# Second attention: VectorE's heads written out, the joining sum on GpSimd, quotients formed in the last stage

## What is computed

```
xn = layernorm(x)
q, k, v = split(xn @ w_qkv)                 # B = 4, N = 256 in the reference's names; here 1 x 2048 rows, 16 heads of 64
out = softmax(rotate(q) @ rotate(k).T / 8) @ v          # per head
x = x + out @ w_out + b_out + ffn(xn)
ffn: h = silu(xn @ w1 * s1) * (xn @ w2 * s2)
     h = gelu(h @ h1 * s); h = gelu(h @ h2 * s); h @ w3 * s3
```

## Time and profile before

| | before |
|---|---|
| median of 3 runs | 3438.32 us |
| profiled execution | 3422.39 us |
| its span, first to last instruction | 3420.6 us |
| PE busy | 2997.9 us (88%) |
| DVE busy | 2827.3 us (83%) |
| ACT busy | 3045.0 us (89%) |
| POOL busy | 2475.8 us (72%) |

### The profile page before, as it was taken

How to read it: one execution, slowest core, us unless ns; L and a number is a source line. 1 busy time by engine, 2 the same in 40 slices (tenths; PEclk the granted TensorE clock), 3 DMA queues, 4 the chain that set the end, 5 groups by cost and what they waited for, 6 DMA issues and landing times. The chain is left out here.

```text
span 3420.6 us, 60293 instructions
## 1 busy us (share of the span) xinstructions
PE 2997.9 (88%) x19523; PEld 1263.5 (37%) x19523; DVE 2827.3 (83%) x4260; ACT 3045.0 (89%) x3039; POOL 2475.8 (72%) x1581
## 2 busy tenths in 40 slices
PE   6888888888888888888887978998989889899899
PEld 3222122212222122221222434555555555555547
DVE  7989999999998999999998988887878778788321
ACT  3999999999999999999997766998989889899942
POOL 5888888888888888888875545576767667677650
PEclk9788778877788778877787989999999999999999
DMA  2000000000000000000001360110000111000000
GB/s 74 7 8 7 7 0 7 7 7 2 5 7 7 7 0 7 7 7 0 7 10 40 130 192 26 40 37 26 26 26 26 32 39 32 26 26 26 23 20 13
DMA packets 59521, 85.32 MB, mean 25 GB/s; under 512 B 10064, under 2 KB 45904, under 8 KB 58960
## 3 DMA queue, kind: packets, MB, share of 16 engines
q1 hardware_dynamic: 59344, 82.93, 8.4%
HBM read 52.31 MB, written 30.54 MB: 24 GB/s over the span
## 5 line engine op out<-in xcount | busy, mean ns | idle before, releaser
L1266 POOL TENSOR_TENSOR lo<-pr,hi 128x1024 f16<-128x1024 f32 x384 | 820.3, 2163 | 388.5 <-ACT hi L1438 384.0
L1327 DVE TENSOR_REDUCE mx<-mx_ps 128x1 f32<-128x512 f32 x1024 | 661.3, 685 | 157.8 <-PE mx_ps L1491 156.7
L1461 ACT ACTIVATE pr<-s_ps 128x1024 f32<-128x1024 f32 x512 | 534.6, 1044 | 130.3 <-PE s_ps L1522 116.8
L1438 ACT ACTIVATE hi<-pr 128x1024 f16<-128x1024 f32 x512 | 551.0, 1077 | 0.0
L713 ACT ACTIVATE wt<-wt,theta_bias 128x2048 f32<-128x2048 f32 (+2 forms) x160 | 482.5, 3016 | 3.7 <-DVE wt L563 3.0
L722 ACT ACTIVATE wt<-wt 128x2048 f32<-128x2048 f32 x256 | 485.3, 1896 | 0.5
L501 POOL TENSOR_TENSOR wt<-base,wt 128x1024 f32<-128x1024 f32 x192 | 455.7, 2373 | 16.0
L501 POOL TENSOR_TENSOR wt<-vb,wt 128x1024 f32<-128x1024 f32 x192 | 455.4, 2372 | 16.0
L1541 PE MATMUL pv_ps<-vh,hi 128*128 128x129 f16 x4096 | 427.8, 221 | 34.7 <-DVE lo L1371 25.6
L1491 PE MATMUL mx_ps<-ka,qa 128*128 128x512 f16 x1024 | 367.6, 389 | 72.7 <-DVE mx L1327 57.9
L1541 PE MATMUL pv_ps<-vh,lo 128*128 128x65 f16 x4096 | 413.9, 193 | 0.0
(11 more groups left out here) (210 smaller groups left out, 5114.8 us busy)
## 6 DMA issues: line engine op xcount, KB each, us to landing
qk<-stg SPq DMA_DIRECT2D x6, 2048.0 KB, 10.8
vh<-v SPq DMA_DIRECT2D x16, 520.0 KB, 3.4
qa<-qk SPq DMA_DIRECT2D x16, 512.0 KB, 3.6
ka<-qk SPq DMA_DIRECT2D x32, 256.0 KB, 4.8
v<-v_st SPq DMA_DIRECT2D x3, 2080.0 KB, 7.9
qst<-parts_dram SPq DMA_DIRECT2D x144, 32.0 KB
kst<-parts_dram SPq DMA_DIRECT2D x144, 32.0 KB
qk<-stg SPq DMA_DIRECT2D x4, 1024.0 KB, 7.8
```

What stands on the lines that cost most here:

```text
L1266: eng.tensor_tensor(lo[:, i % NHL, :, :], pr_slot(i), hi[:, i % NHL, :, :], ALU.subtract).then_inc(lo_done, 1)
L1327: eng.tensor_reduce(mx4[:, q // NCH, q % NCH:q % NCH + 1], mx_ps[:, q % 2, :], AX.X, ALU.max)\
L1438: eng.activation(hi[:, i % NHL, :, :], pr_slot(i), ACT.Copy).then_inc(hi_done, 1)
L1461: eng.activation(pr_slot(i), s_ps[:, i % 2, :, :], ACT.Exp, scale=SM).then_inc(exp_done, 1)
```

## The change

Four edits. The DVE loop over pairs of heads, and POOL's loop over heads, are Python loops now, so that their streams are written out in full. The joining sum is POOL's: it reads `sums` and writes `attn1`, and it stands in POOL's queue behind the low part of steps 5, 13, 21 and 23; ACT's `take` waits for it and for the reciprocal. ACT's `divide` is gone. The reciprocals of all heads are kept (`rden`, 128 x 16 x 16), and DVE multiplies each row tile of `attn1` by them in the last stage, in 16 instructions of 128 x 1024, before the transposes. So that memory allows it, `h1` (8 KB in each partition) isn't kept through the attention any more but fetched at the start of the last stage, ahead of `h2`, `w3` and `wo`.

```diff
@@ stage_attention1, sync @@
-                                 (sb["sc"][:, 2, :], io["h1_s"]), (sb["sc"][:, 3, :], io["h2_s"]),
-                                 (sb["h1"][:, :, :], io["h1_t"].rearrange("(k p) o -> p k o", p=P))):
+                                 (sb["sc"][:, 2, :], io["h1_s"]), (sb["sc"][:, 3, :], io["h2_s"])):
@@ vector, take @@
                     eng.wait_ge(sums_taken, n_ + 2)
-                    eng.reciprocal(rden[:, :].unsqueeze(2), sums[:, :, HD1:HD1 + 1])
-                    eng.tensor_tensor(sums[:, :, 0:HD1], sums[:, :, 0:HD1], sums[:, :, HD1 + 1:VN], ALU.add)\
-                       .then_inc(div_ready, 1)
+                    eng.reciprocal(rden[:, c * TS:(c + 1) * TS, h:h + 1], sums[:, :, HD1:HD1 + 1])\
+                       .then_inc(rden_ready, 1)
@@ vector @@
-                with eng.Fori(1, H // 2 - 1) as g:
+                for g in range(1, H // 2 - 1):
                     one(g, 0)
                     one(g, 1)
@@ gpsimd @@
-                with eng.Fori(0, H) as h:
-                    for i in range(STEPS):
-                        if not on_vector(i):
-                            low(eng, h, i, lo_gpsimd)
+                def join(h, c):
+                    eng.wait_ge(sums_taken, NS * h + c + 2)
+                    eng.tensor_tensor(attn1[:, c * TS:(c + 1) * TS, h * HD1:(h + 1) * HD1], sums[:, :, 0:HD1],
+                                      sums[:, :, HD1 + 1:VN], ALU.add).then_inc(attn_ready, 1)
+                for h in range(H):
+                    for i in range(NLG):
+                        low(eng, h, i, lo_gpsimd)
+                        if i % KP == SUM + 1 and h + i // KP >= 1:
+                            join(h if i >= KP else h - 1, (i // KP - 1) % NS)
+                    join(h, NS - 2)
+                join(H - 1, NS - 1)
@@ scalar @@
-                def divide(h, c):
-                    eng.wait_ge(div_ready, NS * h + c + 1)
-                    for j in range(TS):
-                        last = eng.activation(attn1[:, c * TS + j, bass.ds(h * HD1, HD1)], sums[:, j, 0:HD1],
-                                              ACT.Identity, scale=rden[:, j:j + 1])
-                    last.then_inc(attn_ready, 1)
                 def take(h, c):
                     eng.wait_ge(attn_ready, NS * h + c + 1)
+                    eng.wait_ge(rden_ready, NS * h + c + 1)
@@ stage_output @@
+                sp.dma_start(h1[:, :, :], io["h1_t"].rearrange("(k p) o -> p k o", p=P)).then_inc(h1_loaded, 16)
@@ gpsimd @@
-                eng.wait_ge(weights_loaded, 16 * 7)
+                eng.wait_ge(h1_loaded, 16)
                 split(h1, h1_hl, 0)
@@ vector, behind the 16 casts of L1802 @@
+                for k in range(NT):
+                    by_head = attn1[:, k, :].rearrange("p (h e) -> p h e", h=H)
+                    eng.tensor_tensor(by_head, by_head, rden[:, k, :].unsqueeze(2).to_broadcast([P, H, HD1]),
+                                      ALU.mult).then_inc(divided, 1)
@@ tensor, turn @@
+                    eng.wait_ge(divided, k + 1)
```

More of the change, by code:

```diff
@@ L1232, in stage_attention1 @@
         mrow = t("mrow", [NT, P], F16)
-        sums, rden = t("sums", [P, TS, VN]), t("rden", [P, TS])
+        sums, rden = t("sums", [P, TS, VN]), sb["rden"]
         s_ps = ctx.enter_context(nc.psum_tensor("s_ps", [P, 2, 2, SC], F32))
@@ L1243, in stage_attention1 @@
         pv_done = sem("pv_done1")
-        sums_taken, div_ready, attn_ready = sem("sums_taken"), sem("div_ready"), sem("attn_ready1")
+        sums_taken, rden_ready, attn_ready = sem("sums_taken"), sem("rden_ready"), sem("attn_ready1")
         rest_loaded, v_loaded = sem("rest_loaded"), sem("v_loaded")
@@ L1463, in one @@
                             take(h - 1 if i == SUM else h, (i // KP - 1) % NS)
-                        if i % KP == SUM + 2 and not (first and i == SUM + 2):
-                            divide(h - 1 if i == SUM + 2 else h, (i // KP - 1) % NS)
                         if i >= 1 or not first:
@@ L1470, in one @@
                         take(h, NS - 1)
-                        divide(h, NS - 1)
                 one(0, first=True)
@@ L1589, in _ @@
                 eng.sem_inc(attn_ready, 1)
+                eng.sem_inc(rden_ready, 1)
                 eng.sem_inc(mrow_loaded, 16)
@@ L1605, in stage_output @@
 def stage_output(nc, io, sb):
-    base, attn1, xn2T, ident = sb["base"], sb["attn1"], sb["xn2T"], sb["ident"]
+    base, attn1, rden, xn2T, ident = sb["base"], sb["attn1"], sb["rden"], sb["xn2T"], sb["ident"]
     MO = INNER // P
@@ L1620, in sem @@
             return ctx.enter_context(nc.semaphore(name))
-        w1, w2, h1, sc = sb["w1"], sb["w2"], sb["h1"], sb["sc"]
+        w1, w2, sc = sb["w1"], sb["w2"], sb["sc"]
+        h1 = t("h1", [P, M1, F1])
         h2 = t("h2", [P, M1, F1])
@@ L1639, in stage_output @@
         low_ready, h_high, h_split = sem("low_ready1"), sem("h_high"), sem("h_split")
-        turned, aT_ready = sem("turned_e"), sem("aT_ready")
+        turned, aT_ready, divided = sem("turned_e"), sem("aT_ready"), sem("divided")
         loaded, weights_loaded = sem("loaded_e"), sb["weights2_loaded"]
+        h1_loaded = sem("h1_loaded")
         gate_ps, up_ps, sil_ready = sem("gate_ps1"), sem("up_ps1"), sem("sil_ready1")
@@ L1665, in _ @@
             def _(eng):
-                eng.wait_ge(weights_loaded, 16 * 7)
+                eng.wait_ge(weights_loaded, 16 * 6)
                 for k in range(NM):
@@ L1840, in program @@
         with ExitStack() as layer1:
-            sb |= dict(attn1=keep(layer1, "attn1", [P, NT, INNER]), w1=keep(layer1, "w1", [P, F1]),
+            sb |= dict(attn1=keep(layer1, "attn1", [P, NT, INNER]), rden=keep(layer1, "rden", [P, NT, H]), w1=keep(layer1, "w1", [P, F1]),
                        w2=keep(layer1, "w2", [P, F1]), sc=keep(layer1, "sc", [P, 4, M1]),
-                       h1=keep(layer1, "h1", [P, M1, F1]),
                        weights2_loaded=layer1.enter_context(nc.semaphore("weights2_loaded")))
```

## The result

After the change the kernel takes 3348.84 us (median of 4 runs, 3346.46 to 3351.49), beside 3432.65 us before on the same chip (4 runs, 3424.49 to 3439.79): ratio 0.9759, 95% interval 0.9736 to 0.9782. That is 84 us off where 101 were forecast, and 3349 where 3337 was. The profiled executions say more: 3346.5 us against 3322 forecast in that frame.

What follows compares the result with a forecast made beforehand. In a head PE paces steps 2 to 26, ACT the rest. 40.8 + 44.8 + 2.1 + 2.0 + 14.3 + 0.6 - 0.5 - 3.2 = 100.9 us off: 3321.5 profiled, plus 16: 3337; range 3308 to 3370.

Steps and rivals of the forecast that it cites:

- The loop written out: DVE's loop over heads: five backward branches go with the stops behind them, 40.8 us off.
- The join off DVE: Heads 1 to 14: PE's three waits behind joins lose 3.2 us a head, 44.8 off, bounds 22 and 53.
- 2.1 and 2.0 beside it: 2.1 us off in the 72.16 us head with the 3.93 us join; 2.0 off for two joins in head 0.
- The join on POOL: Heads 1 to 14: a join takes 0.75 us on POOL, ends 0.5 and 1.6, hidden, 0 lost.
- That just closes: In a head POOL needs 24 x 2.14 + 3 x 0.75 = 53.6 us before weigh(23), which PE wants at 53.65.
- The rival of POOL's pace: weigh(23) waits for POOL, a head takes 63.6 + 3X for a join of X; 3361 us at 1.3, chance 0.13.
- The division: Step 30 on ACT, heads 0 to 14: 0.95 us each, 14.3 off, other end 6; steps 6, 14, 22 nothing.
- What is late next: Head start: ka's landing holds PE's first bank up to 0.5 us, taken in by PE's 0.75 us wait before weigh(0).
- The head of 65.9 us: Forecast length of each of 14 heads: 70.07 - 3.2 - 0.95 us.
- The last stage, +3.2: h1 lands 5.6 us after the stage's start, PE's seventh gate comes 3.2 us later, bounds 2.2 and 5.6.
- The 16 multiplications: Last stage, DVE: 1.2 us each, 19.4 in all, under PE's 41.6 us of the second hidden layer, 0 lost.
- the waits change owner: PE's waits go half to DVE's reciprocal and ka's landing; 22 + 8 less gained, 3367 us, chance 0.10.

Runs made afterwards that it cites:

- e2_low_first: The changed kernel with VectorE's last low half of the head before made ahead of the first bank of maxima in step 2; 3331.15 us, ratio 0.9722.
- e3_pause: The changed kernel with four small activations, results unused, put back on ScalarE in step 30 where the division was; 3344.24 us, ratio 0.9768.
- e5_q_split: e2_low_first with the load of qa cut in two, only its first 512 columns ahead of ka on the queue; 3324.52 us, ratio 0.9682.

## Why the prediction was right, and where it was short

The range held the time and the direction was clear; the size was 17 us short in the medians and 25 in the profiled frame. By its own steps:

- **The loop written out, 40.8.** Right in its reason: no "issue" wait is left on DVE, and head 1 was a fair sample of straight code. Alone it gave 26 us of span, because three heads turned long by a late load and the collision, and one by a long join and a lower clock; without those 12 us it is 38.4.
- **The join off DVE, 44.8 with 22 and 53 as ends, and 2.1 and 2.0 beside it.** Right: 41 by ratios, 52 by spans for putting it back, though with the division gone and the loop written out, so that the joins fall elsewhere.
- **The join on POOL, nothing lost at 0.75.** Right, and for more than the stated reason. "That just closes" was too narrow: low parts come every 2.09 us (eight in 16.7) and not 2.14, a join every 0.60. So 24 x 2.09 + 3 x 0.60 = 52.0 where 53.6 was reckoned, and with two joins each it still closes by 0.7. The rival of POOL's pace, 63.6 + 3X, falls by the doubled join: its threshold lies above 1.2 us of join, not at the 0.77 at which it gives 65.9. The same 1.6 us explains, I think, most of head 15, which was 3 us shorter where none was forecast; no run tested that.
- **The division, 15 x 0.95.** This is the step that fell short. Its price is right (67.00 against 66.05 with and without). So is the remark that the load of ka would come 0.5 late and that the wait of step 4 takes it in: that much of the ka wait cost nothing in e2_low_first. It left out two things. The first stands between the two. "What is late next" was asked of PE alone. The same 0.95 us brings POOL's first low part forward, which waits only for ACT, while DVE's last low half waits behind a bank that waits for a load that doesn't move with ACT: the load is issued when the scores end and lands when it lands. Before, DVE was 0.31 us ahead of POOL; so much, and not the 0.5 of PE, was the room. Past it DVE's half took 1.99 us in place of 0.69, and the head became 67.86 and not 65.9. The pause on ACT that made the heads shorter shows it without any edit to DVE or the load. The second is the load itself: the forecast took its landing, 4.9 us after the issue, from one head. In the changed kernel the later of the two loads of ka lands 4.9 to 6.6 us after its issue, and the trace of before already had 4.8 to 6.3, those above 5.3 all in heads in which DVE stopped at its branch. Over 13 heads 28.4 us are missing (885.05 less 13 x 65.9): the order gave back 15.8 of them, the earlier load 8.4 more, and 4.2 stay open. The first two together are twice what the division was worth in these heads.
- **The head of 65.9 us.** Met, at 66.05 to 66.2, by six heads of 13 once the order of the two instructions is fixed, and by ten once the load comes earlier too.
- **The last stage, +3.2.** A misread row. The seventh gate needs product 4, but 3257.64 in the earlier trace rows is the sixth gate of the stage; the seventh comes a pair, 1.72 us, later. 3260.9 less 3259.4 is 1.5, and 1.59 was measured. Part of that match is luck: in the changed kernel, as before, the first pairs of gates ran at a granted clock of 0.67, so PE came late to the seventh. In e2_low_first, e3_pause and e5_q_split they ran at 1.00, and the same wait is 3.46 to 3.56 us.
- **The 16 multiplications, nothing.** Right, 1.27 us each and no wait behind them.

The rival "the waits change owner" named the right kind (ka's landing) but priced it at the 0.5 us of PE's own delay and gave it 0.10. The Trainium skill ("SBUF — State Buffer", "SBUF: two separate sides") has the rule that decides it: of an instruction of VectorE with two SBUF inputs and one of GpSimd that reads SBUF, whichever starts first blocks the other for its whole length. The prediction weighed it only for the joins that it moved; the 1.99 us of a low half that nobody had touched is the same rule at work: POOL's low part of 2561.40 takes 2.1 us, to 2563.5, and DVE's half, 0.6 us of work, ends at 2564.08. The ends 2.67 to 2.69 us after POOL's start in twelve heads agree with it, and a slowing in proportion would not give one end for all starts. By it one should have listed each two-input operation of DVE within a microsecond of one of POOL's, and asked which of them the change would bring to the other side.

## What to carry to other kernels

When an engine on the path gets faster, list not only what it waits for next but which instructions of other engines it releases earlier, and whether one of these shares something with an instruction that another, unmoved event releases. The distance between the two starts in the trace (here 0.31 us) is the room that there is, and swapping one pair in a queue can be worth more than the work that was removed. A stretch that gets shorter when a pause is put in has such a pair in it. And count from the stage's first row when a row is named by its number.

## What the runs showed of the hardware

- A two-input operation of 128x512 on DVE takes 0.69 us alone. Started 0.3 to 1.6 us behind POOL's 2.1 us low part it takes 2.4 to 1.1 and ends 2.67 to 2.69 us after POOL's start in each of 18 heads of three kernels. A join on POOL beside DVE's low halves takes up to 1.14 us instead of 0.64; so the blocking goes both ways.
- A load of the same size at the same place of the program lands between 4.9 and 6.6 us after its issue (14 heads of the changed kernel). In the two heads in which PE stood 2.1 or 2.2 us for it the granted clock was 0.98 on average: PE was busy 67.1 us and not 65.6. DVE is busy only 52.7 us there, so they have no collision: 66.05 + (2.1 - 0.5) + 1.5 makes the 69.2 us.
- Where 384 KB fewer stand ahead of a load in the queue, it was early enough in 11 heads of 14 and at most 1.1 us late in the rest.
- Instructions written out for twelve heads and run once each came without a stop for "issue" on DVE, where a backward branch had cost 4.75 us and more. POOL's showed none either, but neither had its loop before.
